# Value products of a windowed attention, two heads to a matrix product, in a software-pipelined transformer pass

## The chip, the cores and the metric

The kernel runs on one core of a Trainium2 chip, in one launch. The time is that of the device in microseconds. The core has a matrix engine (PE; its weight loads are listed apart as PEld), a vector engine (DVE), a scalar engine (ACT), GpSimd (POOL), and a sync engine (SP) that here only issues DMAs. Each engine works through its own list of instructions in order and waits on semaphores of the others.

## The reference, cut to what matters

The whole program has four stages in sequence. Nearly three quarters of the time is the last one, a transformer of 6 layers on 16 sequences of 256 tokens with 128 features, in float32, 16 heads of 64 features, and attention within windows of 32 queries on 64 keys (the window before and the own one):

```python
q, k, v = split(x @ Wqkv)                     # 16 heads of 64
q, k = l2norm(q) * qs, l2norm(k) * ksc        # then rotary, with a scale
sim = einsum('bhwie,bhwje->bhwij', bq, bk2) * 8
sim = where(mask, -max, sim)
attn = softmax(sim)
out = einsum('bhwij,bhwje->bhwie', attn, bv2) # the value products: 32 queries x 64 keys x 64 features
x = out @ Wo + x
x = ffn_layer(shift_tokens(x), ...) + x       # layernorm, gated gelu, 341 hidden features
```

## The kernel before

A **pass** of `transformer_phase` works on six sequences at once, each at another stage. Its letters are A (projection of q and k, norms, rotary: `project`, `square`, `rotate`, `squares`, `roots`), R (scaling and transposes of q and k, and v: `unit_scale`, `turn`, `turned`, `values`), B (scores, softmax, values: `scores`, `less_max`, `exponent`, `sums`, `by_sum`, `probs`, `attend`, `heads_out`), Dn (the last head group of the sequence before, then the output projection: `combine`, `attention_add`), C (the feed-forward: `back`, `statistics`, `root`, `normal`, `normed`, `affine`, `hidden`, `gelu`, `contract`, `ffn_add`), and F (for the 16 sequences of the last layer alone: `last`, `last_stats`, `last_root`, `last_normal`, the final layer norm). There are 96 sequences times layers, and so 101 passes, of which 5 fill and 5 drain the pipe. The order of the work within a pass is written out by hand, once for each engine, in the lists below `for A, R, B, Dn, C, F in passes()`. All waits are on semaphores that count finished steps.

The heads come in 4 groups of 4. For one group of one sequence:

- `scores(n, g)` (line 1521) makes 32 small products into the bank pS, for 8 windows by 4 heads. Head j goes to columns 32j of the array, and rows 0 or 64 by its parity.
- DVE subtracts the maximum (`less_max`), ACT takes the exponential (`exponent`), DVE sums (`sums`), POOL divides (`by_sum`).
- `probs(n, g)` on PE (line 1549) transposes the result into the bank pT, and ACT copies it to PT (line 1413).
- `attend(n, g)` on PE (line 1568) makes the value products. The windows are taken in the order [1, 3, 5, 7, 0, 2, 4, 6]; the b-th of them lies in rows 0 to 63 of V and PT when b is even, in rows 64 to 127 when odd. The even ones write the bank pO, the odd ones pT. For each window there are four products, one per head: V of the head is the stationary operand (64 rows by 64 columns), PT of the head streams (64 rows by 32 columns). Heads of even number use columns 0 to 63 of the array, odd ones 64 to 127, so that the array works as four tiles of 64 by 64. Before the first of them PE runs a `nop` (`at_rest`).
- `heads_out(n, g)` on ACT (line 1421) copies pO and pT (both halves of the output, 128 partitions by 256 elements each) to oT. Only when that is done may `probs` of the next group overwrite pT.
- `combine(n)` on PE (line 1581) projects oT into pO, and `attention_add` (line 1286) adds that to the residual. `attend(n + 1, 0)` waits for it, since it writes pO.

Every float32 product appears in the trace as two weight loads and two matrix instructions; the 32 products of one `attend` are 64 pairs. Transposes are one pair each.

Of the kernel before, what the change touches and what calls it, by code (L numbers as in the profile page):

```python
# [987 lines left out]
def transformer_phase(nc, I, X, ident, out, layers):  # L988
# [11 lines left out]
    with ctx:  # L1000
# [45 lines left out]
        pOV = [x[:, 0:L].rearrange("p (c t k) -> p c t k", c=2, t=T) for x in (pO, pT)]  # L1046
# [24 lines left out]
        a_ov, p_wo = Steps(ctx, nc, "act_ov", "ov*2"), Steps(ctx, nc, "pe_wo", "wo")  # L1071
# [10 lines left out]
        def passes():  # L1082
            for m in range(NP + 5):
                yield [n if 0 <= n < NP else None for n in range(m, m - 5, -1)] + [m - 5 if m - 5 >= NP - NSEQ else None]
# [62 lines left out]
        def _(e):  # L1147
# [48 lines left out]
            for A, R, B, Dn, C, F in passes():  # L1196
                unit_scale(R, 0)
                root(C)
                rotary_add(A, 0)
                unit_scale(R, 1)  # L1200
                by_sum(B, 0)
                rotary_add(A, 1)
                last_root(F)
                unit_scale(R, 2)
                by_sum(B, 1)
                unit_scale(R, 3)
                rotary_add(A, 2)
                by_sum(B, 2)
                by_sum(B, 3)
                rotary_add(A, 3)  # L1210

        @block.vector
        def _(e):
# [130 lines left out]
            for A, R, B, Dn, C, F in passes():  # L1344
                if A is not None and starts(A):
                    tables(A)
                less_max(B, 0)
                statistics(C)
                rotate(A, 0)
                normal(C)  # L1350
                squares(A, 0)
                less_max(B, 1)
                sums(B, 0)
                rotate(A, 1)
                squares(A, 1)
                roots(A if A is not None else NP if R == NP - 1 else None)
                last_stats(F)
                attention_add(Dn)
                less_max(B, 2)
                sums(B, 1)  # L1360
                hidden(C, 0)
                rotate(A, 2)
                less_max(B, 3)
                squares(A, 2)
                last_normal(F)
                sums(B, 2)
                hidden(C, 1)
                hidden(C, 2)
                sums(B, 3)
                rotate(A, 3)  # L1370
                ffn_add(C)
                squares(A, 3)

        @block.scalar
        def _(e):
# [39 lines left out]
            def heads_out(n, g):  # L1415
                if n is None:
                    return
                i = 4 * n + g
                e.wait_ge(p_pv.sem, p_pv.at("pv", i))
                for h in range(2):  # L1420
                    e.activation(oT[:, 2 * g:2 * g + 2, :].rearrange("p c (t k) -> p c t k", t=T)[:, :, :, KEYS * h:KEYS * (h + 1)],  # L1421
                                 pOV[h], ACT.Copy).then_inc(a_ov.sem, 1)
# [32 lines left out]
            for A, R, B, Dn, C, F in passes():  # L1455
                square(A, 0)
                masked(B, 1)
                probs(Dn, 3)
                turned(R, 0)
                exponent(B, 0)  # L1460
                heads_out(Dn, 3)
                square(A, 1)
                masked(B, 2)
                values(R, 0)
                affine(C)
                exponent(B, 1)
                gelu(C, 0)
                gelu(C, 1)
                probs(B, 0)
                square(A, 2)  # L1470
                turned(R, 1)
# [3 lines left out]
                turned(R, 2)  # L1475
                exponent(B, 2)
                probs(B, 1)
                values(R, 1)
                exponent(B, 3)
                square(A, 3)  # L1480
                heads_out(B, 1)
                turned(R, 3)
                probs(B, 2)
                if B is not None and B + 1 < NP:
                    masked(B + 1, 0)
# [3 lines left out]
        def _(e):  # L1489
# [62 lines left out]
            def attend(n, g):  # L1552
# [10 lines left out]
                for b, w in enumerate(ORDER):  # L1563
                    r = KEYS * (b % 2)
                    for j in range(4):
                        h = 4 * g + j
                        c = HD * (j % 2)
                        x = e.matmul(pOV[b % 2][c:c + HD, j // 2, w // 4, WIN * (w % 2):WIN * (w % 2 + 1)],  # L1568
                                     V[n % 2][r:r + KEYS, w // 4, 1 - w % 2, h * HD:(h + 1) * HD],
                                     PT[i % 2][r:r + KEYS, (b // 2) * P + 32 * j:(b // 2) * P + 32 * j + 32],  # L1570
                                     start=True, stop=True, tile_position=(r, c))
# [88 lines left out]
            for A, R, B, Dn, C, F in passes():  # L1660
                scores(B, 0)
                project(A, 0)
                back(C)
                probs(Dn, 3)
                turn(R, 0)
                scores(B, 1)
                attend(Dn, 3)
                project(A, 1)
                values(R, 0)
                normed(C)  # L1670
                combine(Dn)
                probs(B, 0)
                hidden(C, 0)
                project(A, 2)
                scores(B, 2)
                turn(R, 1)
                hidden(C, 1)
                last(F)
# [4 lines left out]
                values(R, 1)  # L1683
                project(A, 3)
                hidden(C, 2)
                attend(B, 1)
                turn(R, 3)
                probs(B, 2)
                contract(C)
# [87 lines left out]
```

## Time and profile before

| | |
|---|---|
| median of 3 runs | 4465.24 us (4464.75 to 4467.26) |
| the profiled execution | 4472.1 us |
| its span in the trace | 4470.2 us |
| mean granted TensorE clock, share of full | 0.971 |
| PE busy | 4226.6 us, 95% |
| DVE busy | 3363.1 us, 75% |
| ACT busy | 2458.3 us, 55% |
| POOL busy | 2133.5 us, 48% |

The stages before the transformer take about 1,170 us; the transformer's passes take the rest. The shares of DVE, ACT and POOL are averages over both and are higher in the transformer.

### The profile page before, as it was taken

To read this page: it belongs to the slowest core of one execution; us is meant where nothing else is said; L and a number is where in the kernel's file an instruction comes from. 1 tells how busy PE (TensorE), PEld (TensorE's weight loads), DVE (VectorE), ACT (ScalarE), POOL (GpSimd) and SP (SyncE) were. 2 spreads that over 40 slices of the span, in tenths; PEclk is the share of its full clock that TensorE was granted. 3 is DMA by queue.
4 is the path that set the end of the run, shared out by engine and by line. 5 is a ranking of instruction groups with operands and counts; after the bars stand their busy time and mean duration, and the time that the engine had idled before them with its cause. 6 is when DMAs were issued, how large, how long until landed. Compare 5 with 4: busy or idle time off the path is not lost.

```text
span 4470.2 us, 146512 instructions
## 1 busy us (share of the span) xinstructions
PE 4226.6 (95%) x64231; PEld 3077.6 (69%) x64231; DVE 3363.1 (75%) x7591; ACT 2458.3 (55%) x4522; POOL 2133.5 (48%) x1317
## 2 busy tenths in 40 slices
PE   5999999988699999999999999999999999998997
PEld 3777776666377777777777777777777777766665
DVE  5444444444698898888988888888888889887784
ACT  2111111111367676776776776767767767666663
POOL 1000000001466666666666666666666666665552
PEclk8999999999799999999999999999999999999998
DMA  3000000000011111111111111111111111111110
GB/s 128 1 1 1 1 1 1 1 1 1 23 40 39 34 50 54 39 36 39 53 50 35 40 39 48 50 39 39 42 51 45 39 34 49 54 37 37 34 34 24
DMA packets 70594, 152.46 MB, mean 34 GB/s; under 512 B 14524, under 2 KB 43079, under 8 KB 69575
## 3 DMA queue, kind: packets, MB, share of 16 engines
q1 hardware_dynamic: 69958, 143.09, 10.8%
q8 instruction: 509, 8.34, 0.8%
q14 instruction: 127, 1.03, 0.1%
HBM read 27.69 MB, written 2.10 MB: 7 GB/s over the span
## 4 chain that ended last, share of the span: by engine, by line
PE 63%; DVE 4%; ACT 3%; issue 3%; POOL 2%; POOLq 0%; DVEq 0%
PE pQ L1537 14%; PE pS L1521 9%; PE pM L1603 7%; PE pO L1581 6%; PE pM L1592 6%; PE pC L1637 5%; PE pO L1568 4%; PE pT L1568 4%; PE pT L1549 3%; PE pC L1647 3%; ACT sq L1406 2%; POOL rot L1166 1%; POOL rot L1174 1%; ACT pS L1390 1%; DVE rot L1256 1%
## 5 line engine op out<-in xcount | busy, mean ns | idle before, releaser
L1174 POOL TENSOR_TENSOR rot<-rot,m 128x1024 f32<-128x1024 f32 x384 | 905.1, 2357 | 397.3 <-DVE m L1260 397.3
L1166 POOL TENSOR_TENSOR rot<-rot,rn 128x1024 f32<-128x1024 f32 x384 | 732.8, 1908 | 245.9 <-DVE rn L102 245.9
L1406 ACT ACTIVATE sq<-pQ 128x1024 f32<-128x1024 f32 x384 | 393.7, 1025 | 463.1 <-PE pQ L1537 463.1
L1183 POOL TENSOR_TENSOR E<-E,rc 128x512 f32<-128x512 f32 x384 | 400.5, 1043 | 352.4 <-DVE rc L1246 352.1
L1256 DVE TENSOR_TENSOR rot<-pQ,tabl 128x1024 f32<-128x1024 f32 x384 | 461.8, 1203 | 36.0 <-ACT sq L1406 35.4
L1568 PEld LDWEIGHTS pO<-PT,V 64*64 64x64 f32 x12288 | 389.9, 135 | 132.8 <-issue 124.1
L1521 PEld LDWEIGHTS pS<-kT,qT 64*32 64x32 f32 x24576 | 369.6, 108 | 141.3 <-issue 105.3
L1260 DVE TENSOR_TENSOR m<-pQ,tabl 128x1024 f32<-128x1024 f32 x384 | 466.2, 1214 | 0.0
L1271 DVE TENSOR_REDUCE n<-sq 128x16 f32<-128x1024 f32 x384 | 464.1, 1209 | 0.0
L1568 PE MATMUL pO<-PT,V 64*64 64x32 f32 x12288 | 432.0, 221 | 29.7 <-issue 27.3
L1521 PE MATMUL pS<-kT,qT 64*32 64x64 f32 x24576 | 434.6, 220 | 22.9 <-issue 12.6
L1592 PE MATMUL pM<-ident,rot 128*128 128x128 f32 x3072 | 422.2, 281 | 23.8 <-POOL rot L1166 23.8
L786 POOL MEMSET c_xn<- 128x48 f32 x1 | 0.1, 147 | 926.6 <-POOLq L493 926.6
L1568 PE MATMUL pT<-PT,V 64*64 64x32 f32 x12288 | 434.7, 221 | 0.0
L1537 PE MATMUL pQ<-wq,xs 128*128 128x512 f32 x768 | 385.9, 625 | 10.5 <-DVE m L1260 9.1
L1568 PEld LDWEIGHTS pT<-PT,V 64*64 64x64 f32 x12288 | 392.1, 133 | 0.0
L1537 PE MATMUL pQ<-wk,xs 128*128 128x512 f32 x768 | 364.9, 598 | 9.0 <-DVE m L1260 9.0
L1592 PEld LDWEIGHTS pM<-ident,rot 128*128 128x128 f32 x3072 | 337.5, 142 | 46.3 <-POOL rot L1166 29.3
L1603 PE MATMUL pM<-wv,xs 128*128 128x512 f32 x768 | 365.1, 598 | 0.0
L1581 PE MATMUL pO<-oT,wo 128*128 128x256 f32 x1536 | 348.6, 380 | 0.6 <-ACT oT L1421 0.4
L1232 DVE TENSOR_REDUCE mx<-pS 128x8 f32<-128x512 f32 x384 | 262.7, 684 | 82.8 <-PE pS L1521 82.6
L1581 PEld LDWEIGHTS pO<-oT,wo 128*128 128x128 f32 x1536 | 285.1, 191 | 36.6 <-ACT oT L1421 1.2
(221 smaller groups left out, 7842.2 us busy)
## 6 DMA issues: line engine op xcount, KB each, us to landing
V<-V SPq DMA_DIRECT2D x192, 384.0 KB, 3.5
xs<-XT SPq DMA_DIRECT2D x192, 64.0 KB, 2.9
V<-V SPq DMA_DIRECT2D x96, 128.0 KB, 3.3
ys<-XT SPq DMA_DIRECT2D x192, 64.0 KB, 2.1
wq<-in_wqkv SPq DMA_DIRECT2D x6, 512.0 KB, 4.8
wk<-in_wqkv SPq DMA_DIRECT2D x6, 512.0 KB, 4.0
wv<-in_wqkv SPq DMA_DIRECT2D x6, 512.0 KB, 5.5
wo<-in_wo SPq DMA_DIRECT2D x6, 512.0 KB, 3.9
```

Source lines behind the costliest of these rows:

```text
L1166: e.tensor_tensor(r, r, rn[b % 2][:, c:c + HEADS].unsqueeze(2).to_broadcast([P, HEADS, HD]), ALU.mult)\
L1174: e.tensor_tensor(rot[j % RING][:, :], rot[j % RING][:, :], m2[:, :, :].rearrange("p h d -> p (h d)"), ALU.add)\
L1256: e.tensor_tensor(rot[j % RING][:, :].rearrange("p (h d) -> p h d", d=HD), pQ[:, :].rearrange("p (h d) -> p h d", d=HD), tl[:, t, 2 * w, : ...
L1260: e.tensor_tensor(m2[:, :, :].rearrange("p h (b d) -> p h b d", b=2), pQ[:, :].rearrange("p (h b d) -> p h b d", b=2, d=HD // 2)[:, :, ::- ...
L1271: e.tensor_reduce(n2[:, c:c + HEADS], sq[:, :].rearrange("p (h d) -> p h d", d=HD), AX.X, ALU.add)\
L1406: e.activation(sq[:, :], pQ[:, :], ACT.Square).then_inc(a_sq.sem, 1)
L1521: x = e.matmul(pS[32 * j:32 * j + 32, b * KEYS:(b + 1) * KEYS], q[r:r + HD, h // 2, WIN * w:WIN * (w + 1)], k[r:r + HD, h // 2, WIN * w:WI ...
L1537: x = e.matmul(pQ[:, i * 512:(i + 1) * 512], xs[n % 3][:, t * P:(t + 1) * P], wqkv[w][:, i * 512:(i + 1) * 512], start=True, stop=True)
L1568: x = e.matmul(pOV[b % 2][c:c + HD, j // 2, w // 4, WIN * (w % 2):WIN * (w % 2 + 1)], V[n % 2][r:r + KEYS, w // 4, 1 - w % 2, h * HD:(h + ...
L1581: x = e.matmul(pO[:, 0:L], wo[:, c, :], oT[:, c, :], start=c == 0, stop=c == N // P - 1)
L1592: x = e.transpose(pM[i][:, c * P:(c + 1) * P], rot[j % RING][:, (4 * i + c) * P:(4 * i + c + 1) * P], ident[:, :])
L1603: e.matmul(pM[i][:, :], xs[n % 3][:, t * P:(t + 1) * P], wqkv[2][:, i * 512:(i + 1) * 512], start=True, stop=True)\
```

## The change

`attend` makes one product for two heads where it made two. The stationary operand is V of heads 2c and 2c + 1 side by side, 64 rows by 128 columns; PT of both heads streams, 64 rows by 64 columns. The output is 128 partitions (head, feature) by 64 (head, query), of which the two blocks whose head is the same on both sides are wanted; the other two are computed too and are left in the bank. There are 16 products for a group (32 pairs in the trace) of twice the width on both operands. The array works as two tiles of 64 rows by 128 columns. pO and pT are filled whole, 512 columns each, not half.

`heads_out` copies the diagonal blocks alone: four copies of 64 partitions by 256 elements where there were two of 128 partitions by 256 (`a_ov` counts four steps a group, not two).

Then the lists of all four engines are put in another order. On PE, `back(C)` comes first, `last(F)` moves up from behind `hidden(C, 1)` to behind `attend(Dn, 3)`, which itself comes ahead of `scores(B, 1)`; `combine(Dn)` and `hidden(C, 0)` come ahead of `probs(B, 0)`; `values(R, 1)` and `contract(C)` move to between `attend(B, 1)` and `probs(B, 2)`. On DVE `statistics(C)` is first, `last_stats(F)` moves ahead of `squares(A, 0)`, and `last_normal(F)` behind `ffn_add(C)`; on POOL `last_root(F)` moves behind `rotary_add(A, 2)`. No DMA is changed, and SP's list stays as it is.

```diff
-        pOV = [x[:, 0:L].rearrange("p (c t k) -> p c t k", c=2, t=T) for x in (pO, pT)]
+        pairs = [x[:, :].rearrange("p (c t v h k) -> p c t v h k", c=2, t=T, v=2, h=2) for x in (pO, pT)]
...
-        a_ov, p_wo = Steps(ctx, nc, "act_ov", "ov*2"), Steps(ctx, nc, "pe_wo", "wo")
+        a_ov, p_wo = Steps(ctx, nc, "act_ov", "ov*4"), Steps(ctx, nc, "pe_wo", "wo")
...                       # POOL, passes
+                by_sum(B, 0)
                 unit_scale(R, 1)
-                by_sum(B, 0)
                 rotary_add(A, 1)
-                last_root(F)
                 unit_scale(R, 2)
                 by_sum(B, 1)
                 unit_scale(R, 3)
                 rotary_add(A, 2)
+                last_root(F)
...                       # DVE, passes
+                statistics(C)
                 if A is not None and starts(A):
                     tables(A)
                 less_max(B, 0)
-                statistics(C)
                 rotate(A, 0)
                 normal(C)
+                last_stats(F)
                 squares(A, 0)
...
-                last_stats(F)
                 attention_add(Dn)
                 less_max(B, 2)
                 sums(B, 1)
+                rotate(A, 2)
                 hidden(C, 0)
-                rotate(A, 2)
                 less_max(B, 3)
                 squares(A, 2)
-                last_normal(F)
...
                 ffn_add(C)
+                last_normal(F)
                 squares(A, 3)
...                       # ACT, heads_out
-                for h in range(2):
-                    e.activation(oT[:, 2 * g:2 * g + 2, :].rearrange("p c (t k) -> p c t k", t=T)[:, :, :, KEYS * h:KEYS * (h + 1)],
-                                 pOV[h], ACT.Copy).then_inc(a_ov.sem, 1)
+                o = oT[:, 2 * g:2 * g + 2, :].rearrange("p c (t u v k) -> p c t u v k", t=T, u=2, v=2)
+                for u in range(2):
+                    for h in range(2):
+                        r = slice(HD * h, HD * (h + 1))
+                        e.activation(o[r, :, :, u, :, :], pairs[u][r, :, :, :, h, :], ACT.Copy).then_inc(a_ov.sem, 1)
...                       # ACT, passes
                 square(A, 0)
+                probs(Dn, 3)
                 masked(B, 1)
-                probs(Dn, 3)
                 turned(R, 0)
+                heads_out(Dn, 3)
                 exponent(B, 0)
-                heads_out(Dn, 3)
                 square(A, 1)
-                masked(B, 2)
                 values(R, 0)
                 affine(C)
+                masked(B, 2)
                 exponent(B, 1)
                 gelu(C, 0)
+                probs(B, 0)
                 gelu(C, 1)
-                probs(B, 0)
+                turned(R, 1)
                 square(A, 2)
-                turned(R, 1)
                 gelu(C, 2)
                 masked(B, 3)
                 heads_out(B, 0)
-                turned(R, 2)
                 exponent(B, 2)
                 probs(B, 1)
-                values(R, 1)
+                turned(R, 2)
+                if B is not None and B + 1 < NP:
+                    masked(B + 1, 0)
                 exponent(B, 3)
                 square(A, 3)
                 heads_out(B, 1)
+                values(R, 1)
+                probs(B, 2)
                 turned(R, 3)
-                probs(B, 2)
-                if B is not None and B + 1 < NP:
-                    masked(B + 1, 0)
                 heads_out(B, 2)
...                       # PE, attend
-                    for j in range(4):
-                        h = 4 * g + j
-                        c = HD * (j % 2)
-                        x = e.matmul(pOV[b % 2][c:c + HD, j // 2, w // 4, WIN * (w % 2):WIN * (w % 2 + 1)],
-                                     V[n % 2][r:r + KEYS, w // 4, 1 - w % 2, h * HD:(h + 1) * HD],
-                                     PT[i % 2][r:r + KEYS, (b // 2) * P + 32 * j:(b // 2) * P + 32 * j + 32],
-                                     start=True, stop=True, tile_position=(r, c))
+                    for c in range(2):
+                        h = 4 * g + 2 * c
+                        x = e.matmul(pairs[b % 2][:, c, w // 4, w % 2, :, :].rearrange("p h k -> p (h k)"),
+                                     V[n % 2][r:r + KEYS, w // 4, 1 - w % 2, h * HD:(h + 2) * HD],
+                                     PT[i % 2][r:r + KEYS, (b // 2) * P + 2 * WIN * c:(b // 2) * P + 2 * WIN * (c + 1)],
+                                     start=True, stop=True, tile_position=(r, 0))
...                       # PE, passes
+                back(C)
                 scores(B, 0)
                 project(A, 0)
-                back(C)
                 probs(Dn, 3)
                 turn(R, 0)
+                attend(Dn, 3)
+                last(F)
                 scores(B, 1)
-                attend(Dn, 3)
                 project(A, 1)
+                normed(C)
                 values(R, 0)
-                normed(C)
                 combine(Dn)
+                hidden(C, 0)
                 probs(B, 0)
-                hidden(C, 0)
-                project(A, 2)
                 scores(B, 2)
                 turn(R, 1)
+                project(A, 2)
                 hidden(C, 1)
-                last(F)
                 attend(B, 0)
                 turn(R, 2)
                 scores(B, 3)
                 probs(B, 1)
-                values(R, 1)
                 project(A, 3)
                 hidden(C, 2)
                 attend(B, 1)
+                values(R, 1)
+                contract(C)
+                probs(B, 2)
                 turn(R, 3)
-                probs(B, 2)
-                contract(C)
                 attend(B, 2)
```

## Rows read from the trace of the kernel before

**Rows 1.** The page, busy time, share of the span, instructions.
```profile
PE 4226.6 (95%) x64231; PEld 3077.6 (69%) x64231; DVE 3363.1 (75%) x7591; ACT 2458.3 (55%) x4522; POOL 2133.5 (48%) x1317
```

**Rows 2.** Sums over a window: stretch, length, busy of each engine, granted clock, DMA.
```profile
1300.00:4400.00 3100.00, 3039.46 (x57073) 2221.51 (x57072) 2705.48 (x4950) 2136.44 (x3846) 1989.57 (x1199) 0.99 0.15 42
```

**Rows 3.** Timeline of PE, one pass: start, length, instructions, count; the next pass's start.
```profile
2416.12 1.10 PE L1521 MATMUL pS<-kT,qT 64*32 64x64 f32 x64
...
2418.97 0.38 PE L1614 MATMUL pC<-ident,ys 128*128 128x128 f32 x2
2419.18 0.60 PE L1549 MATMUL pT<-ident,E 128*128 128x128 f32 x4
2419.62 1.04 PE L1592 MATMUL pM<-ident,rot 128*128 128x128 f32 x8
2420.74 1.10 PE L1521 MATMUL pS<-kT,qT 64*32 64x64 f32 x64
2421.77 0.25 PE L1568 MATMUL pO<-PT,V 64*64 64x32 f32 x2
2421.80 0.25 PE L1568 MATMUL pT<-PT,V 64*64 64x32 f32 x2
2421.85 0.23 PE L1568 MATMUL pO<-PT,V 64*64 64x32 f32 x2
...
2422.70 0.23 PE L1568 MATMUL pT<-PT,V 64*64 64x32 f32 x2
2422.85 1.98 PE L1537 MATMUL pQ<-wq,xs 128*128 128x512 f32 x4
...
2449.10 1.10 PE L1521 MATMUL pS<-kT,qT 64*32 64x64 f32 x64
```

**Rows 4.** Timeline of PE, `combine` of the 2nd, 83rd and 94th of 96 sequences.
```profile
1264.91 3.62 PE L1581 MATMUL pO<-oT,wo 128*128 128x256 f32 x16
...
3951.63 3.62 PE L1581 MATMUL pO<-oT,wo 128*128 128x256 f32 x16
...
4373.79 3.62 PE L1581 MATMUL pO<-oT,wo 128*128 128x256 f32 x16
```

**Rows 5.** Timeline of PE in an earlier stage: 128-column loads, 8 columns streamed.
```profile
303.33 1.92 PE L702 MATMUL b_pm<-b_rd,b_it 128*128 128x8 f32 x16 [0.57 <-ACT b_xcT L633]
305.11 1.10 PE L713 MATMUL b_pg<-b_wd,b_it 128*128 128x512 f32 x2
```

**Rows 6.** Weight loads by shape (groups of instructions; instructions of one line).
```profile
L1568 PEld LDWEIGHTS pT<-PT,V 64*64 64x64 f32 x12288 | 392.1, 133 | 0.0
...
L475 PEld LDWEIGHTS a_pz<-a_wzo,a_z x64: 182/188/335, 37.6 to 82.8; 64*128 64x128 f32 x64
...
L1581 PEld LDWEIGHTS pO<-oT,wo x16: 190/190/192, 2426.5 to 2429.6; 128*128 128x128 f32 x16
```

**Rows 7.** Timeline of ACT in the pass of rows 3.
```profile
2419.16 1.03 ACT L1406 ACTIVATE sq<-pQ 128x1024 f32<-128x1024 f32 x1 [2.24 <-PE pQ L1537]
2420.09 0.60 ACT L1390 ACTIVATE pS<-mask 128x512 f32<-128x512 f32 x1
...
2423.00 0.38 ACT L1421 ACTIVATE oT<-pO 128x256 f32<-128x256 f32 x1 [0.31 <-PE pT L1568]
2423.28 0.38 ACT L1421 ACTIVATE oT<-pT 128x256 f32<-128x256 f32 x1
```

**Rows 8.** Timelines of PE, DVE and POOL, a pass of the last layer.
```profile
3999.90 0.25 PE L1568 MATMUL pO<-PT,V 64*64 64x32 f32 x2 [2.07 <-issue]
...
4002.06 1.97 PE L1592 MATMUL pM<-ident,rot 128*128 128x128 f32 x8 [0.89 <-POOL rot L1166]
...
3997.86 0.42 DVE L1328 TENSOR_TENSOR X<-X,pM 128x256 f32<-128x256 f32 x1 [2.23 <-PE pM L1657]
...
3999.27 0.42 DVE L1286 TENSOR_TENSOR XT<-pO,XT 128x256 f32<-128x256 f32 x1
...
3999.44 0.70 POOL L84 TENSOR_TENSOR fyr<-fve,yh 128x2 f32<-128x2 f32 x1 [6.65 <-DVE fve L1332]
```

## The prediction

> **What bounds the kernel now.** I read the page first: PE is busy for 95% of the span [rows 1]. That alone says little, since the ends of matrix instructions are modelled and pipelined ones overlap. So I took the sums over the stretch in which the passes run evenly [rows 2]: of 3,100 us PE is busy 98%, DVE 87% (2705/3100), ACT 69%, POOL 64%, at a granted clock of 0.99. Then the timeline of PE over one pass [rows 3]. The reader is to see that each group of instructions starts where the last one stops: `scores` 1.03 us from its start to the next group's (2420.74 to 2421.77), `attend` 1.08 (2421.77 to 2422.85), and the next pass 32.98 us after this one (2416.12 to 2449.10). There is no gap to fill: an instruction added on PE adds its time to the pass, and one taken away gives it back until DVE, with about 28.8 us of work a pass, is reached. Last I took the start of `combine` in the 2nd, 83rd and 94th sequence [rows 4]: 81 passes of 33.17 us on average, 0.19 over the even one, then 11 passes of 38.38. So the passes with the final layer norm (F) have stalls of 5.4 us each, and the earlier ones 15 us (81 x 0.19) in all.
>
> **What bounds one `attend`.** This decides the case. The 64 pairs start in rounds of four: two into pO at 2421.77, two into pT at 2421.80, the next two into pO at 2421.85 [rows 3]. So the four tiles work at once, one pair on each, and from the first round to the last half of the 16th 0.93 us pass, 0.060 a round (0.93/15.5). What takes 0.060 us in a tile? A pair is a load of 64 columns and 32 streamed columns. For wide loads there is a row: 16 pairs with 128 columns loaded and only 8 streamed take 1.78 us, 0.111 each [rows 5]. With 8 columns streamed, that can only be the load. So a load takes some 0.87 ns a column; 64 columns then make 0.056 us, about the round that is seen. `attend` is bound by its weight loads, four at a time.
>
> **The change, part by part.**
>
> *The products.* A group has 32 pairs instead of 64, but on two tiles instead of four: still 16 rounds. Each round now loads 128 columns, 0.111 us, and streams 64, which fits beneath. 16 x (0.111 - 0.060) = 0.82 us more a group, on the path. Does a load with 64 rows cost what one with 128 rows does? The trace has both shapes: 188 ns against 190, and 133 ns for 64 by 64 [rows 6]. So the length goes with columns. 6 x 16 x 4 = 384 groups: 384 x 0.82 = +315 us. Bounds: no growth, if wide loads on half the rows ran at twice the rate; 32 x 0.111 - 0.93 = 2.6 us a group, if the two row tiles did not overlap. I take 0.82, since row tiles do overlap in rows 3, where the program issues eight pairs for rows 0 to 63 before it turns to rows 64 to 127 and the trace shows both from the first round on. Within that, 0.7 to 1.0 (269 to 384 us).
>
> The rows say that the load is the bound. The Trainium skill (TensorEngine Tiling, Theoretical Speedup) gives each dimension of 64 or less a factor of two, so that giving up the tiling of columns would double the whole of `attend`, 1.08 to 2.16 us. By it, as an estimate, the sum would be 100 us higher than mine; the trace of before can't show which is nearer.
>
> *The copies.* ACT starts a second copy 0.28 us after the first [rows 7], so two more cost 0.56 us a group, 2.2 us a pass. ACT has 0.69 x 33 = 22.8 us of work in a pass that will have near 37; it is not a bound. What counts is how soon a `probs` may write pT. After an `attend`, ACT starts 0.15 us later (2422.85 to 2423.00), four copies take 3 x 0.28 + 0.38 = 1.22, and PE wakes about 0.2 us after a release (DVE's add ends at 3999.69, `attend` starts at 3999.90 [rows 8]): 1.6 us. The tightest place in the new order is `attend(B, 0)` to `probs(B, 1)`, with `turn` (1.12) and `scores` (1.03) between, 2.15 us. The others have `back`, `scores` and `project`, or `values` and `contract`. So I cost the copies at nothing; without that cover they would cost 0.56 us a group, 215 us.
>
> *The new order, even passes.* One place gets worse. `attend(Dn, 3)` now stands right behind `turn(R, 0)`; `back` and `scores(B, 1)` no longer lie between. It needs ACT's copy of pT, which follows `square(A, 0)`, and that waits for `project(A, 0)`. Counted from the end of that (2418.97): the square starts 0.19 later, the next instruction of ACT 0.93 after it, and takes 0.60, as a copy of the same shape does [rows 7], then 0.2 to wake PE: 1.92 us. PE has `probs` (0.44) and `turn` (1.12) [rows 3], 1.56. A stall of 0.36 us, 96 times: +35 us (bounds 0 and 0.6, 0 to 58). Behind `attend(Dn, 3)` wait `scores(B, 1)` and `project(A, 1)`; both their inputs are ready by then. PE also goes once more into and out of small tiles. Eight transposes take 1.12 us in front of `scores` where 8 x 0.111 = 0.89 would be their loads, so a change of shape costs some 0.1 to 0.2: +14 us (96 x 0.15; bounds 0 and 22). I walked the rest of the lists through with the durations of the trace and found every other input ready: the pass is 3.3 us longer on PE and hardly on DVE and POOL. SP's list is the same. Its copies of V wait for `values(R, 1)`, which is later by `hidden`, `attend` and a `project`, but are wanted only at `attend(B, 0)` of the next pass, more than 15 us on; the queues' share is 0.15 [rows 2]. The layers' stalls of 15 us (DVE late at a layer's first pass) should largely go into the longer pass: -10 us (bounds 0 and 15).
>
> *The new order, last layer.* There DVE waits 2.23 us for `last`, then adds and takes statistics, and `attend(B, 0)`, which needs `attention_add` behind them, starts 2.07 us late; POOL waits 6.65 us for the variance, so that its scalings come late, and `turn` loses another 0.89 [rows 8]. After the change `last(F)` is done before DVE comes to `last_stats(F)`, and `last_root(F)` stands behind the scalings that `turn` waits for. What is late next? `values(R, 0)` wants the bank that `last` used; it comes two groups of PE later, behind `scores` and `project`. Of the 11 x 5.4 = 59 us I give back all but the cost of `last` itself with its change of shape, 0.4 us a pass: -55 us (bounds -30 and -59).
>
> **The sum.** Against the profiled execution of 4472.1 us: + 315 + 35 + 14 - 10 - 55 = 4771. Its median stands 6.9 us lower (4465.24), so 4764 us, 6.7% slower.
>
> **The rivals.**
>
> *Pairs cost by number, not by width (other side; 0.06).* For it: `scores`, with 64 pairs of other shapes, takes 1.03 us, and `attend` 1.08, as if each pair cost 16 ns. Then 32 pairs take 0.51 and `attend` 0.66 us with its 0.15 of end, 0.42 less: -161 instead of +315, 4288 us. Against it: the pairs within a round start closer together than the rounds, and rows 5 show 111 ns for a pair with hardly anything streamed. It decides where `attend` grows by less than 0.04 us a group, for the other terms come to -16 us. The Trainium skill (TensorE: Matmul & The Clock Gate, "Wait — 56ns, not 53.3ns?") states a floor of about 25 ns between starts. By that rule 64 pairs would take 1.6 us; the trace has 1.08 and so disagrees.
>
> *No change within the measurement (0.01).* The growth would have to fall on 0.02 to 0.06 us; 4456 to 4474 us.
>
> *ACT comes late (0.09).* `attend` grows as I say, but `heads_out` stands behind a `square` (1.03 us) or an exponential and its table load when PE wants pT or PT. The spare time of 0.55 us (2.15 - 1.6) is then used up and about half a microsecond lost, at two places of each pass: 96 us more, 4860. For it: two more copies in a row at each of the four places. Against it: ACT idles over 10 us of a pass.
>
> *The row tiles don't overlap (0.04).* Each wide load holds the whole array: +998 instead of +315, 5447 us. Against it: rows 3, as above.
>
> **How the numbers follow.** The forecast has 0.80. Its own range comes from the bounds: 269 to 384 for the products, 0 to 58 and 0 to 22 for stalls and shapes, -30 to -59 and 0 to -15 for what is regained. All at one end would give 4660 or 4899; they will hardly all fall on one side, so 4690 to 4880, which takes in ACT coming late and leaves out the other rivals and the outermost parts of this one. A change of 0.2% (9 us) is about what a measurement of this kernel can tell from none. Faster: 0.06 by the count of pairs and 0.01 for a mere part of it; within 0.2%: 0.01; slower: 0.92.
>
> **What would show it.** In the timeline of PE, 32 pairs in two alternating tiles, 0.11 us a round, and 1.9 us from the start of `attend` to the next group, where I count on 1.08 + 0.82. The first product of `attend(Dn, 3)` about 0.4 us behind the last transpose. An even pass of 36.8 us. Passes of the last layer of 37.2 us, with no wait of PE behind `last`. Weight loads of `attend` near 188 ns each. The prediction is wrong if a round takes 0.06 us (loads go by rows too), or 0.22 (no overlap), if `probs(B, 1)` waits for ACT, or if the passes of the last layer keep their stalls.

## The result

| | before | after |
|---|---|---|
| median of 3 runs | 4465.24 us | 4765.68 us (4764.26 to 4766.56) |
| profiled execution, span | 4472.1, 4470.2 us | 4765.68, 4763.9 us |
| mean granted TensorE clock | 0.971 | 0.980 |

The ratio is 1.0672, with a 95% interval of 1.0654 to 1.0690. The forecast was 4764 us. In the experiments below the kernel before took 4467 to 4470 us (medians of 7 runs), so differences of 5 us are read as none.

The page's busy times after, to be held against [rows 1]:

```profile
PE 4550.7 (96%) x51943; PEld 3409.7 (72%) x51943; DVE 3444.2 (72%) x7591; ACT 2824.0 (59%) x5290; POOL 2135.6 (45%) x1317
```

PE has 12,288 pairs fewer and is busy 324 us longer. The timeline of PE over the part of a pass in which `attend(Dn, 3)` lies, to be held against [rows 3]:

```profile
2399.96 0.44 PE L1615 MATMUL pC<-ident,ys 128*128 128x128 f32 x2
2400.32 1.10 PE L1523 MATMUL pS<-kT,qT 64*32 64x64 f32 x64
...
2403.61 1.04 PE L1593 MATMUL pM<-ident,rot 128*128 128x128 f32 x8
2405.03 0.29 PE L1569 MATMUL pO<-PT,V 64*128 64x64 f32 x1 [0.38 <-ACT PT L1413]
2405.04 0.32 PE L1569 MATMUL pT<-PT,V 64*128 64x64 f32 x1
2405.16 0.27 PE L1569 MATMUL pO<-PT,V 64*128 64x64 f32 x1
2405.20 0.27 PE L1569 MATMUL pT<-PT,V 64*128 64x64 f32 x1
2405.27 0.27 PE L1569 MATMUL pO<-PT,V 64*128 64x64 f32 x1
2405.32 0.27 PE L1569 MATMUL pT<-PT,V 64*128 64x64 f32 x1
2405.38 0.27 PE L1569 MATMUL pO<-PT,V 64*128 64x64 f32 x1
...
2406.98 1.10 PE L1523 MATMUL pS<-kT,qT 64*32 64x64 f32 x64
```

One pair into pO and one into pT alternate, and each tile's next pair comes 0.11 us after its last (2405.16, 2405.27, 2405.38), where a round took 0.060 before. An `attend` lasts 1.95 to 1.98 us to the next group's start (2405.03 to 2406.98), not 1.08. Ahead of it PE waits for ACT's copy: eight transposes and the wait take 1.42 us (2403.61 to 2405.03). In the passes up to 4400 us that is the one wait of PE for another engine that the trace names (total, times, longest):

```profile
PE pO L1569 <- ACT PT L1413: 32.2, 84, 0.4
```

`combine` of the 2nd, 83rd and 94th sequence on PE's timeline, as in [rows 4]:

```profile
1265.44 3.62 PE L1582 MATMUL pO<-oT,wo 128*128 128x256 f32 x16
...
4261.00 3.62 PE L1582 MATMUL pO<-oT,wo 128*128 128x256 f32 x16
...
4668.16 3.62 PE L1582 MATMUL pO<-oT,wo 128*128 128x256 f32 x16
```

81 passes now take 2995.56 us, 36.98 each (33.17 before); the even one is 36.97, so next to nothing is left of the 15 us by which single passes before were longer than the even one (upsets, below). The 11 passes with the final layer norm take 407.16 us (422.16 before): ten of 37.34 us and a last of 33.8, in which A is empty already. Of the 293.7 us that the span grew, 308.8 came in the 81 passes, and 15.0 went in the 11.

The weight loads of `attend` by shape, as in [rows 6] (busy time and mean ns of one behind the bar):

```profile
L1569 PEld LDWEIGHTS pT<-PT,V 64*128 64x128 f32 x6144 | 727.6, 187 | 0.0
L1569 PEld LDWEIGHTS pO<-PT,V 64*128 64x128 f32 x6144 | 714.8, 188 | 141.6 <-issue 141.6
```

They are 187 and 188 ns long, as the one row of that shape in [rows 6] had it.

### The profile page after: what moved, and what is told of

Same layout as the page of the kernel before. It is cut to its first block, busy times and chain, and to the rows that moved or that the text cites. A ratio compares the mean times of both kernels' runs of the same rounds, so it can differ in the third digit from the quotient of the medians.

```text
span 4763.9 us, 122704 instructions
## 1 busy us (share of the span) xinstructions
PE 4550.7 (96%) x51943; PEld 3409.7 (72%) x51943; DVE 3444.2 (72%) x7591; ACT 2824.0 (59%) x5290; POOL 2135.6 (45%) x1317
## 3 DMA queue, kind: packets, MB, share of 16 engines
q14 instruction: 132, 1.08, 0.1%
## 4 chain that ended last, share of the span: by engine, by line
PE 71%; ACT 4%; DVE 1%; issue 1%; POOL 0%; POOLq 0%; DVEq 0%
PE pQ L1539 15%; PE pO L1569 10%; PE pS L1523 8%; PE pM L1604 7%; PE pO L1582 7%; PE pT L1569 6%; PE pM L1593 6%; PE pC L1638 5%; PE pT L1551 3%; PE pC L1648 3%; ACT sq L1406 2%; ACT PT L1413 1%; PE pC L1615 1%; PE pC L1623 0%; ACT oT L1424 0%
## 5 line engine op out<-in xcount | busy, mean ns | idle before, releaser
L1569 PEld LDWEIGHTS pO<-PT,V 64*128 64x128 f32 x6144 | 714.8, 188 | 141.6 <-issue 141.6
L1569 PE MATMUL pO<-PT,V 64*128 64x64 f32 x6144 | 765.0, 275 | 39.9 <-ACT PT L1413 39.9
L1569 PE MATMUL pT<-PT,V 64*128 64x64 f32 x6144 | 780.7, 277 | 0.0
L1569 PEld LDWEIGHTS pT<-PT,V 64*128 64x128 f32 x6144 | 727.6, 187 | 0.0
L1424 ACT ACTIVATE oT<-pO 64x256 f32<-64x256 f32 x768 | 290.8, 379 | 306.1 <-PE pT L1569 285.4
L1523 PE MATMUL pS<-kT,qT 64*32 64x64 f32 x24576 | 422.3, 218 | 0.7 <-ACT kT L1433 0.7
L1593 PE MATMUL pM<-ident,rot 128*128 128x128 f32 x3072 | 411.1, 277 | 9.5 <-POOL rot L1166 9.3
```

What stands on the lines that cost most here:

```text
L1523: x = e.matmul(pS[32 * j:32 * j + 32, b * KEYS:(b + 1) * KEYS], q[r:r + HD, h // 2, WIN * w:WIN * (w + 1)], k[r:r + HD, h // 2, WIN * w:WI ...
L1569: x = e.matmul(pairs[b % 2][:, c, w // 4, w % 2, :, :].rearrange("p h k -> p (h k)"), V[n % 2][r:r + KEYS, w // 4, 1 - w % 2, h * HD:(h + ...
L1593: x = e.transpose(pM[i][:, c * P:(c + 1) * P], rot[j % RING][:, (4 * i + c) * P:(4 * i + c + 1) * P], ident[:, :])
```

## The experiments

### What a round costs: stream half, load half, one tile

`e3_stream_half` leaves the load at 128 columns and streams the first head's 32 alone; the second head's values are left out, and `heads_out` copies the first head's block in their place.

```diff
-    x = e.matmul(pairs[b % 2][:, c, w // 4, w % 2, :, :].rearrange("p h k -> p (h k)"),
+    x = e.matmul(pairs[b % 2][:, c, w // 4, w % 2, 0, :],
...
-    PT[i % 2][r:r + KEYS, (b // 2) * P + 2 * WIN * c:(b // 2) * P + 2 * WIN * (c + 1)],
+    PT[i % 2][r:r + KEYS, (b // 2) * P + 2 * WIN * c:(b // 2) * P + 2 * WIN * c + WIN],
```

> The new kernel, but each product streams the 32 columns of its first head alone (the second head's values are left out, and its copy takes the first head's block). Loads of 128 columns stay. If the load is the bound: attend stays at 1.98 us and the time at 4760 to 4770. If the streamed columns count, a round falls from 0.111 to 0.056 us and the time to about 4430; if load and stream add up, to 4590.

Measured: 4753.87 us (one run). PE's timeline, the start of one `attend` and the next group:

```profile
2413.32 0.29 PE L1569 MATMUL pO<-PT,V 64*128 64x32 f32 x1
2413.34 0.29 PE L1569 MATMUL pT<-PT,V 64*128 64x32 f32 x1
2413.46 0.27 PE L1569 MATMUL pO<-PT,V 64*128 64x32 f32 x1
2413.47 0.27 PE L1569 MATMUL pT<-PT,V 64*128 64x32 f32 x1
2413.57 0.27 PE L1569 MATMUL pO<-PT,V 64*128 64x32 f32 x1
...
2415.25 0.98 PE L1593 MATMUL pM<-ident,rot 128*128 128x128 f32 x7
```

A round is still 0.11 us, `attend` 1.93 where it was 1.98: half the streaming saves 0.05 us a group, and the time lies 12 us below the changed kernel's, 6 us under the first range of the expectation. But for these 0.05 us the streamed columns lie beneath the loads.

`e4_load_half` leaves the streaming at 64 columns and loads the first head's 64 alone; the copies take that head's block twice.

```diff
-    x = e.matmul(pairs[b % 2][:, c, w // 4, w % 2, :, :].rearrange("p h k -> p (h k)"),
-                 V[n % 2][r:r + KEYS, w // 4, 1 - w % 2, h * HD:(h + 2) * HD],
+    x = e.matmul(pairs[b % 2][0:HD, c, w // 4, w % 2, :, :].rearrange("p h k -> p (h k)"),
+                 V[n % 2][r:r + KEYS, w // 4, 1 - w % 2, h * HD:(h + 1) * HD],
```

> The new kernel, but each product loads the 64 columns of its first head alone (the second head's values are left out, and its copy takes the first head's block) and streams 64 columns, on two tiles of 64 by 64. If the load is the bound and a load goes by its columns: a round falls from 0.111 us to that of 64 columns, 0.056 to 0.06, attend to about 1.1 us, the time to 4420 to 4440 us. If it is giving up two of four tiles that costs, and not the width of a load, nothing changes: 4765.

Measured: 4475.37 us (one run). The end of one `attend` on PE's timeline:

```profile
2400.04 0.22 PE L1569 MATMUL pT<-PT,V 64*64 64x64 f32 x1
2400.04 0.22 PE L1569 MATMUL pO<-PT,V 64*64 64x64 f32 x1
2400.09 0.22 PE L1569 MATMUL pT<-PT,V 64*64 64x64 f32 x1
2400.10 0.22 PE L1569 MATMUL pO<-PT,V 64*64 64x64 f32 x1
2400.15 0.22 PE L1569 MATMUL pT<-PT,V 64*64 64x64 f32 x1
...
2400.36 1.10 PE L1523 MATMUL pS<-kT,qT 64*32 64x64 f32 x64
```

Two tiles, 64 columns loaded and 64 streamed: a round of 0.058 us (the median in a tile; the kernel before has 0.058 too, its 0.060 takes in a longer first round), `attend` 1.13, an even pass of 33.55. On two tiles instead of four, with a load as narrow as before, `attend` takes what it took before. So the width of a load costs, not the number of tiles. The total came some 35 to 55 us above what I expected, and about 31 of them (11 x 2.85) lie in the last layer, whose 11 passes take 36.4 us each and not 33.55; `e8` and `e9` below show why.

`e6_one_row_tile` puts every product on rows 0 to 63; the odd windows' values are left out.

```diff
+                    r = 0
                     for c in range(2):
```

> The new kernel with every product on rows 0 to 63 of V and PT (the odd windows' rows are left out, and the even ones' used in their place). If the two row tiles work at the same time before, 32 loads in one row now take 32 x 0.111 = 3.55 us, attend about 3.75, and the time rises by 384 x 1.77 = 680 us to 5440. If they took turns already, nothing changes: 4765.

Measured: 5910.84 us (one run). An `attend` takes 3.71 us (3028.80 to 3032.51), close to the 3.75 of 32 loads one after the other: in the changed kernel the two row tiles do work at once. But the whole came 470 us over the expectation. PE's timeline, and the sums over three short stretches and one long one (stretch, length, busy times, granted clock, DMA share, GB/s):

```profile
3028.80 0.66 PE L1570 MATMUL pO<-PT,V 64*128 64x64 f32 x4
...
3032.51 0.44 PE L1616 MATMUL pC<-ident,ys 128*128 128x128 f32 x2
3032.88 1.59 PE L1523 MATMUL pS<-kT,qT 64*32 64x64 f32 x64
3034.40 3.12 PE L1539 MATMUL pQ<-wq,xs 128*128 128x512 f32 x4
3037.35 0.60 PE L1551 MATMUL pT<-ident,E 128*128 128x128 f32 x4
```

```profile
3025.00:3030.00 5.00, 5.00 (x32) 3.91 (x31) 1.61 (x2) 3.58 (x8) 4.21 (x2) 1.00 0.32 92
3030.00:3035.00 5.00, 5.00 (x91) 4.49 (x90) 1.40 (x6) 1.52 (x4) 0.70 (x1) 0.83 0.05 14
3035.00:3040.00 5.00, 4.62 (x23) 2.87 (x22) 2.29 (x4) 2.45 (x5) 0.00 (x0) 0.83 0.01 3
...
1300.00:5000.00 3700.00, 3670.82 (x37448) 2841.01 (x37447) 2262.85 (x4017) 2064.14 (x3790) 1648.20 (x987) 0.89 0.10 29
```

After `attend` the four products of `project` take 2.95 us to the next group, against 1.82 elsewhere. The granted clock, 1.00 in the stretch before, is 0.83 over these five microseconds, which is a stay at the lower of its two levels (1.2 of 2.4 GHz) for part of them. What PE did before it fell was 3.7 us of work on half of its rows, with not one gap, the third such stretch in 21 us; behind the first (3011.63 to 3015.34) the clock stayed at 1.00. The passes are 48.8 us long in the middle, where 36.97 and four times 1.73 make 43.9; those 5 us, 96 times, are the surplus. Over the passes the granted clock is 0.89 in `e6` and 1.00 in the changed kernel, with PE busy for 99% of the time in both. As an estimate from that, PE lost 0.11 x 48.8 = 5.4 us a pass to the clock, about what is missing.

### The order alone and the products alone

`e1_order_alone` is the new order with the products and the two copies of before; against the changed kernel:

```diff
-                    for c in range(2):
-                        h = 4 * g + 2 * c
...
+                    for j in range(4):
+                        h = 4 * g + j
+                        c = HD * (j % 2)
...                       # and pOV, "ov*2" and heads_out as before
```

`e2_wide_alone` is the old order with the new products and four copies; against the kernel before:

```diff
-                    for j in range(4):
...
+                    for c in range(2):
+                        h = 4 * g + 2 * c
...                       # and pairs, "ov*4" and heads_out as in the change
```

> The new order with the products and copies of before (64 pairs on four tiles, two copies). If the wider weight loads are the whole loss, attend falls from 1.98 to 1.08 us, an even pass from 36.97 to about 33.4, and the time to 4420 to 4440 us, below the 4465 of before, since the last layer's stalls stay away. If the order costs a good part of the 300 us, the time stays at 4550 or more.

> The order of before with the new products and four copies. By the loads: 384 x 0.9 = 345 us more than before, and the last layer's stalls are back, 4810 us. In that order only one group of transposes (0.95 us) lies between attend(B, 1) and probs(B, 2), while the copies need 0.15 + 1.55 + 0.2 us, so another 0.7 us or so a pass should be lost: 4860 to 4880 us, with PE waiting for ACT's copies ahead of that probs. If the copies are hidden everywhere, 4810.

Measured: `e1` 4506.43 us, 1.0088 of before (1.0071 to 1.0105); `e2` 4873.82 us, 1.0909 (1.0890 to 1.0927). `e2` is where its first reading had it; `e1` lies between its two readings, 66 us above the first. Alone, the products and copies cost 407 us and the order 40.

In `e2` the groups last as they did, but `probs(B, 2)` waits for the copies. PE's timeline:

```profile
2418.52 1.09 PE L1593 MATMUL pM<-ident,rot 128*128 128x128 f32 x8
2420.36 0.63 PE L1551 MATMUL pT<-ident,E 128*128 128x128 f32 x4 [0.74 <-ACT oT L1424]
```

1.84 us from the transposes to `probs`, against 0.95 before: 0.89 us a pass. Beside the wider products the new order is worth 4873.8 - 4765.7 = 108 us, where beside the old ones it costs 40. 37 of them are even passes (37.43 against 36.97: that wait goes, and the one ahead of `attend(Dn, 3)` comes), and 50 the last layer, whose 11 passes take 41.6 us each in `e2`; the rest lies in the filling and draining of the pipe.

In `e1` an even pass is 33.42 us, as expected (0.45 us of waiting ahead of `attend(Dn, 3)`), but the 81 passes lose another 56 us to upsets, and the 11 of the last layer take 36.3 us each. PE's timeline at one upset, and what the DMA queues moved from 1447.5 to 1449.5 us (kind: packets, MB, share):

```profile
1447.79 0.44 PE L1614 MATMUL pC<-ident,ys 128*128 128x128 f32 x2
1448.16 0.87 PE L1521 MATMUL pS<-kT,qT 64*32 64x64 f32 x48
1450.43 0.43 PE L1521 MATMUL pS<-kT,qT 64*32 64x64 f32 x16 [1.40 <-issue]
```

```profile
q1 hardware_dynamic: 143, 0.11, 18.4%
q8 instruction: 1, 0.02, 3.1%
```

PE stops in the middle of one `scores`, after 48 of 64 pairs, where its program has no wait. I counted such stops (more than 0.3 us between two starts within one `scores` or `attend`) and set them beside the packets of queue q8, which carries instructions:

```
kernel                  pairs   stops   us in all   resume after the end of an instruction packet
before                  64      13      15.4        1.25 to 1.54 us
e1_order_alone          64      36      53.1        1.21 to 1.59 us
e8_before_early_last    64      16      18.7        1.25 to 1.59 us
e9_last_normal_early    64      20      21.5        1.25 to 1.53 us
e10_small_fetches       64      35      51.1        1.19 to 1.59 us
e11_two_tables          64      30      42.8        1.19 to 1.58 us
after, e2 to e7         32      0       0
```

Every stop ends 1.2 to 1.6 us behind the end of a packet of 16 KB. Of q8 the pages of before and after say (packets, MB, share):

```profile
q8 instruction: 509, 8.34, 0.8%
q8 instruction: 413, 6.77, 0.6%
```

96 packets fewer, for 24,576 fewer weight loads and matrix instructions: q8 brings PE's instructions, 256 to a packet. With that the trace settles where PE stops. If one counts PE's instructions in it up to each of the 150 stops, the number is always 193 or 194 more than a multiple of 256, and that multiple is 256 times the number of q8's packets that have landed. So each stop lies at the same place in a block of instructions and ends after the next block has come, and at no such place in the passes of any of the 13 kernels does PE go on sooner than 1.18 us behind the end of that block's packet. In the changed kernel the shortest distance is 2.5 us. What makes a packet late is not shown: in `e1` those that end a stop take 0.96 us in the median, the others 1.03, but they begin 3.2 us behind PE's step into the block before, the others 0.76.

`e1` and `e4` have one order, and even passes of 33.42 and 33.55 us; they differ in the pairs of an `attend` (and in the copies), and the one with 32 has no stop.

I first took the stops to lie at the start of layers, and tried two causes.

`e10_small_fetches` is `e1` with the layers' weights not fetched from the second layer on, but for 8 columns of each:

```diff
-    e.dma_start(wqkv[1][:, :], I["wqkv"][A // NSEQ, :, N:2 * N])
+    e.dma_start(wqkv[1][:, 0:8], I["wqkv"][A // NSEQ, :, N:N + 8])
...   # the same for wqkv[0], wqkv[2], wo, w1, w2
```

> The new order with the products of before (4506 us), but the weights of the layers from the second on are not fetched: each of the six transfers a layer brings 8 columns alone, so that later layers use the first one's weights but for those columns. In that kernel PE stops in the middle of a group of scores 35 times, 52 us in all, always at the start of a layer or in the last one, with no wait that the trace names. If the big transfers keep PE's instructions from coming in time, most of these stops vanish and the time falls to 4450 to 4470. If they come from the table work of DVE at a layer's start, nothing changes: 4500 to 4510.

`e11_two_tables` is `e1` with the tables of the first two layers used for all:

```diff
-                if A is not None and starts(A):
+                if A is not None and starts(A) and A < 2 * NSEQ:
```

> The new order with the products of before (4506 us), but the scaled rotary tables are made for the first two layers only and used for the later ones too; the 1.5 us of DVE at the start of layers 3 to 6 is left out. If PE's stops at a layer's start come from late instructions, nothing changes: 4495 to 4510. If they come from DVE being late, as I had it in the prediction, four of five layers lose their stops: 4460 to 4470.

Measured: 4499.50 and 4498.07 us (one run each), with 35 stops of 51 us and 30 of 43 us. Neither was the cause: `e10` is at the lower end of its range for no change, and `e11` within the range that its expectation gave for late instructions. The expectations had the place wrong too: the stops come in bunches mostly 12 to 14 passes apart, while a layer has 16.

### The copies and the wait ahead of `attend(Dn, 3)`

`e5_two_copies` makes two copies a group instead of four; half of what they bring is not a diagonal block.

```diff
-                    for h in range(2):
-                        r = slice(HD * h, HD * (h + 1))
+                    for h in range(1):
+                        r = slice(0, P)
```

> The new kernel with two copies a group in heads_out where it has four: all 128 partitions of one head's columns, so that half of what lands in oT is not a diagonal block. ACT saves 0.8 us a group. If the copies are hidden, as I costed them, the time stays at 4758 to 4768 us. If ACT comes late anywhere, 30 us or more are saved.

Measured: 4760.29 us, 1.0659 of before (1.0641 to 1.0677); an even pass is 36.97 us, to the hundredth that of the changed kernel. The two extra copies cost nothing in the passes; the 5 us in the total are no more than two measurements differ by.

`e7_scores_ahead` puts `scores(B, 1)` back ahead of `attend(Dn, 3)`.

```diff
-                attend(Dn, 3)
-                last(F)
                 scores(B, 1)
+                attend(Dn, 3)
+                last(F)
...                       # ACT
-                probs(Dn, 3)
                 masked(B, 1)
+                probs(Dn, 3)
```

> The new kernel with scores(B, 1) back in front of attend(Dn, 3) and last(F), and masked(B, 1) in front of probs(Dn, 3) on ACT, as before. The wait of 0.45 us ahead of attend(Dn, 3) goes away, 43 us; scores(B, 1) may wait some 0.1 us for the mask: 4722 to 4735 us. If the wait only moves to scores(B, 1) or to project(A, 1), 4755 to 4765.

Measured: 4773.74 us, 1.0683 of before (1.0665 to 1.0701). An even pass is 36.91 us, 0.06 less; the passes of the last layer take 37.65 us where they took 37.34. The total is 9 us above the second reading's range, and against before it can't be told from the changed kernel's 1.0672 (1.0654 to 1.0690). The waits that end on ACT's mask (total, times, longest):

```profile
PEld pS L1523 <- ACT pS L1390: 38.0, 71, 0.5
...
PE pS L1523 <- ACT pS L1390: 21.2, 71, 0.3
```

Now `scores(B, 1)` waits 0.3 us in every pass for `masked(B, 1)`, which stands behind the same `square(A, 0)`. The wait moved, as the second reading had it, and nothing was gained. It hangs on the square, not on which of the two groups comes first.

### The final layer norm

`e8_before_early_last` and `e9_last_normal_early` are the kernel before with the parts of F moved and nothing else. `e9`:

```diff
                 attend(Dn, 3)         # PE
+                last(F)
                 project(A, 1)
...
                 normal(C)             # DVE
+                last_stats(F)
                 squares(A, 0)
...
+                last_normal(F)
                 roots(A if A is not None else NP if R == NP - 1 else None)
...
                 by_sum(B, 0)          # POOL
+                last_root(F)
                 rotary_add(A, 1)
```

`e8` has two of them where the change puts them; against `e9`:

```diff
-                last_normal(F)
                 roots(A if A is not None else NP if R == NP - 1 else None)
...
                 ffn_add(C)
+                last_normal(F)
...
-                last_root(F)          # POOL
                 rotary_add(A, 1)
...
                 rotary_add(A, 2)
+                last_root(F)
```

> The kernel before with nothing changed but the final layer norm's place: last(F) right behind attend(Dn, 3) on PE, last_stats(F) behind normal(C) and last_normal(F) behind ffn_add(C) on DVE, last_root(F) behind rotary_add(A, 2) on POOL. If the stalls of the last layer come from the old place, 11 x 5.4 = 59 us less some 5 to 25 for the work itself, as DVE has little room in a pass of 33 us: 4410 to 4435. If they come from DVE being full in these passes, 4455 to 4465.

> The kernel before with the final layer norm in other places: last(F) right behind attend(Dn, 3) on PE, last_stats(F) behind normal(C) and last_normal(F) just ahead of roots(A) on DVE, last_root(F) behind by_sum(B, 0) on POOL. In the kernel before with last_normal(F) behind ffn_add(C) each of its two instructions took up to 2 us, in the kernel before 0.34, and passes of the last layer 37.2 us. If that is because GpSimd works on its large products at that point, the passes of the last layer now come to 33.5 to 34.5 us, and the time to 4405 to 4425 us. If DVE is simply full there, they stay at 36 to 37: 4435 to 4450.

Measured: `e8` 4444.14 us, 0.9949 of before (0.9932 to 0.9966), passes of the last layer 37.24 us. `e9` 4415.23 us, 0.9879 (0.9862 to 0.9895), passes 34.89 us. It leaves nothing out, and is the fastest kernel here. `e8` lies between its two readings: the old place of F made part of the stalls, and the rest has another cause. `e9` has its time as expected, with passes 0.4 us longer than the range for them.

Between the two lie the places of `last_normal` and `last_root`; what differs in the trace is mainly one thing. DVE's two instructions of `last_normal` in `e8`, and what POOL did then:

```profile
4009.87 4.02 DVE L1340 TENSOR_SCALAR X<-X,fmv,fyr 128x128 f32<-128x128 f32 x2
```

```profile
4009.59 2.36 POOL L1174 TENSOR_TENSOR rot<-rot,m 128x1024 f32<-128x1024 f32 x1 [1.19 <-DVE m L1260]
4011.91 1.90 POOL L1166 TENSOR_TENSOR rot<-rot,rn 128x1024 f32<-128x1024 f32 x1
```

The two took 4.02 us (0.59 in the kernel before, with POOL idle) and were done at 4013.89; POOL's second product ends at 4013.81. Over all 32 of them, by kernel (duration ns min/median/max), first the changed kernel, then `e9`:

```profile
L1340 DVE TENSOR_SCALAR X<-X,fmv,fyr x32: 336/1188/1943, 4283.4 to 4761.3; 128x128 f32<-128x128 f32 x32
```

```profile
L1340 DVE TENSOR_SCALAR X<-X,fmv,fyr x32: 332/345/1484, 3953.1 to 4412.6; 128x128 f32<-128x128 f32 x32
```

Each of these DVE instructions holds on until POOL's has ended: of the 32, 22 last over 0.5 us in the changed kernel, and 22 in `e8`, and every one of them ends 0.08 to 0.09 us behind the end of a POOL product (in `e9` 11 do). In the changed kernel that is hidden, since DVE has room even there: it is busy for 368.7 of 400 us in the last layer. In `e4`, with the same order and a pass of 33.55 us, DVE becomes the bound in the last layer, 36.4 us a pass. The Trainium skill (SBUF — State Buffer, "SBUF: two separate sides") has GpSimd and certain DVE instructions share a pair of ports that one of them holds for its whole instruction; the ends above agree.

## Why the prediction was right

The range held and the mechanism was right. That the number came within 2 us is luck: some terms were off, by +26, +8, -14 and -4 us, and 15 us that I had counted outside the even passes did not come; they made up for each other.

- **`attend` is bound by its weight loads, which go by columns.** Right, and shown two ways: half the streaming takes 0.05 of 1.98 us away (`e3`), half the load 0.85, all but back to the old time (`e4`). The rival of row tiles that don't overlap is out by `e6`: all products on one of them take 3.71 us. The rival that pairs cost by number is out: half as many take 1.8 times as long.
- **Its growth: 0.82 us predicted, 0.87 to 0.90 measured**, some 341 us and not 315 over 384 groups. The round was right (0.112, against 0.111). The end of the group was under-sized: before, the last pair started 0.15 us ahead of the next group [rows 3]; now it is 0.20 (2406.78 to 2406.98), and the first round takes 0.13. The doubling that I set beside it, 1.08 more, was too much.
- **The wait ahead of `attend(Dn, 3)`: 0.36 predicted, 0.45 measured** (1.42 us, against 0.97 for the same transposes ahead of `attend(B, 2)`), 43 and not 35 us. Its cause was right too: the trace names ACT's copy of pT.
- **One more change into and out of small tiles: +14 predicted, none net.** `back` in front of `scores` does take 0.36 us, 0.15 more than before. But the 1.12 us of `turn` in front of `scores(B, 1)`, from which I took the price, held about 0.1 us of waiting for the mask: elsewhere eight transposes ahead of `scores` take 1.02. I read a wait as a cost, and it went with the new order.
- **The upsets: -10 predicted, -14 measured, for the wrong reason.** I had DVE late at a layer's start. The passes of 34 to 35 us in the kernel before are PE's stops inside `scores` (in the 81 passes 11 stops, 12.7 of the 15.3 us), and no kernel with 32 pairs has one. `e11` leaves DVE's work at the start of four layers out, and the stops stay.
- **Copies at nothing**: right in this order (`e5`), though they are longer than I had them. Four take 1.6 us and not 1.22, and ACT is busy 366 us longer, 0.95 us a group and not 0.56; the cover of 2.15 us is still enough. The rival of a late ACT describes the old order, where it costs 0.89 us a pass (`e2`).
- **The last layer: passes of 37.2 predicted, 37.34 measured.** Of the waits in [rows 8] none is left there. That they came from F's place holds in the main: with F moved alone the passes go from 38.38 to 34.89 us (`e9`), against an even one of 32.98. I missed that `last_normal` in its new place takes 3.0 us of DVE where it took 0.6, which the longer pass hides; in passes of 33 us the same place of F gives back 1.1 us a pass (`e8`) and not the 5 that I counted on.
- **What made up for it.** 81 passes grew by 308.8 us where my terms gave 297, but the fill, the drain and the stages before, for which I counted 4 passes of growth or 15 us, came out even; why is not shown.

## What to carry to other kernels

Count the columns of a weight load before you merge small products: two heads in one load of twice the width save no time on a tile where the load is the longer half, and give up the tiles beside it. An order of work is tuned to the length of a pass; measure each half of a change like this one alone, for here the order lost 40 us beside the old products and gained 108 beside the new, and in it lay a gain (another place of the final layer norm) that is worth 1.2% without either, in `e9`. And when a trace shows a group of matrix products torn in the middle with no wait in its program, look at when instructions arrived before you look at data.

## What the runs showed that I had not expected

- PE can run out of instructions. All 150 stops in six kernels lie at one place of a block of 256 instructions and end 1.2 to 1.6 us after the next block's packet of 16 KB, all but three inside `scores`, after stretches in which groups of 64 pairs follow each other closely. The Trainium skill (Runtime: NRT & Kernel Launch, "Instruction fetch mechanics") says that instructions come in blocks of 16 KiB and that crossing into the next is mostly hidden; with 64 pairs in an `attend` it was not, 13 to 36 times. That the late packet is the cause rests on the count of instructions, on this timing and on `e1` against `e4`; no run changed the supply alone, and what delays a packet stays open.
- TensorE's granted clock was 0.89 in the passes of `e6`, whose `attend` puts 3.7 us of gapless loads and products on half of the rows, and 1.00 with both halves at work; some 470 us went that way. PE was busy 99% of the time in both. The clock fell behind some of these stretches and not behind others.
- DVE instructions of 0.34 us lasted up to 2 us beside GpSimd's large products, and ended with them.
- Four tiles of 64 by 64 with 32 columns streamed, and two with 64 streamed, take the same round, 0.058 us.
